# Norms, statistics and low parts in other places of the unit, one bias load a unit earlier, small modulation steps a unit later, in a fused attention and expert block

## The reference, cut to what matters

```python
h = _layernorm(x, axis=-1) * (1 + ca) + sa
q = (hs @ q_w.T + q_b).reshape(B, L, nh, d)        # k and v likewise
qn, kn = _l2norm(q / scale), _l2norm(k / scale)
gv = softplus(hs @ b_w.T + b_b)[..., None] * v
attn = einsum('bnhid,bnhjd->bnhij', qc, kc)        # chunks of 64 tokens
out = einsum('bnhij,bnhjd->bnhid', attn * mask, gvc)
x = x + ga * ((out * silu(hs @ og_w.T)) @ o_w.T + o_b)
h = _layernorm(x, axis=-1) * (1 + cb) + sb
x = x + gb * ffn(h)                                # 16 experts, top 6, and a shared one
```

## Time and profile before

| | |
|---|---|
| time of the kernel before, median of 3 runs | 2174.21 us (2173.03 to 2174.24) |
| the profiled execution's own time | 2172.59 us |
| its span, first to last instruction | 2170.9 us |
| PE busy | 2119.8 us (98%) |
| DVE, ACT, POOL busy | 1193.1 us (55%), 1030.9 us (47%), 525.2 us (24%) |
| mean granted clock of PE | 0.999 |
| the 128 attention units | from about 18 to 1317 us |

### The profile page before, as it was taken

One profiled execution on the slowest core, in us unless ns is written; L12 is line 12 of the kernel. 1 busy time (PEld: TensorE's weight loads), 2 busy tenths in 40 slices (PEclk: granted clock), 3 DMA queues, 4 the chain that ended last, 5 costly groups with the idle time before them and its releaser, 6 DMA issues.

```text
span 2170.9 us, 36048 instructions
## 1 busy us (share of the span) xinstructions
PE 2119.8 (98%) x12463; PEld 1751.7 (81%) x12463; DVE 1193.1 (55%) x2174; ACT 1030.9 (47%) x3301; POOL 525.2 (24%) x541
## 2 busy tenths in 40 slices
PE   7999999999999999999999999999999999999999
PEld 5877878887878887878888887888888888888887
DVE  5556556556556556556555454555555455545554
ACT  5655556566556556556555453333333232333322
POOL 2334344344343344344344441000000000000000
PEclk9999999999999999999999999999999999999999
DMA  7565333254355344445243130442334234223221
GB/s 258 173 225 205 115 120 130 79 161 141 81 142 157 92 164 106 114 139 161 93 142 114 54 127 31 142 168 103 127 110 150 101 112 163 103 90 119 93 97 63
DMA packets 191891, 274.79 MB, mean 127 GB/s; under 512 B 99184, under 2 KB 132960, under 8 KB 191712
## 3 DMA queue, kind: packets, MB, share of 16 engines
q1 hardware_dynamic: 191712, 272.49, 38.8%
HBM read 214.79 MB, written 57.67 MB: 126 GB/s over the span
## 4 chain that ended last, share of the span: by engine, by line
PE 88%; DVE 6%; issue 2%; ACT 2%; DMA 1%; POOL 0%; SPq 0%; DVEq 0%; ACTq 0%; POOLq 0%
PE proj_ps L664 47%; PE out_ps L664 14%; PE av_ps L891 4%; PE s_ps L879 3%; PE s_ps L939 3%; PE av_ps L939 3%; PE qt_ps L939 3%; PE kt_ps L939 3%; PE qt_ps L860 2%; PE kt_ps L865 2%; DVE gated_lo L1497 1%; DVE scores L1472 1%; DMA head_scr<-stage 1%; PE misc_ps L683 1%; DVE xn L1261 1%
## 5 line engine op out<-in xcount | busy, mean ns | idle before, releaser
L664 PE MATMUL proj_ps<-w_qkv,h_t 128*128 128x512 f32 x2304 | 617.6, 406 | 16.3 <-DVE q_sb L1464 5.7
L664 PEld LDWEIGHTS proj_ps<-w_qkv,h_t 128*128 128x128 f32 x2304 | 409.3, 189 | 107.9 <-issue 15.6
L664 PE MATMUL proj_ps<-h_t,w_qkv 128*128 128x512 f32 x1800 | 444.4, 391 | 0.1
L664 PEld LDWEIGHTS proj_ps<-h_t,w_qkv 128*128 128x128 f32 x1800 | 335.7, 188 | 69.2 <-issue 0.7
L621 POOL TENSOR_TENSOR inv_norm<-guarded,minus_half 128x8 f32<-128x8 f32 x128 | 209.9, 1639 | 730.3 <-DVE guarded L1481 730.3
L1182 ACT ACTIVATE w_gate<-v_sb 128x512 fp32r<-128x512 f32 x200 | 126.4, 632 | 314.5 <-DVE v_sb L1539 310.3
L1545 DVE TENSOR_TENSOR w_gate<-v_sb,w_gate 128x512 fp32r<-128x512 f32 x200 | 138.5, 693 | 139.4 <-ACT w_gate L1182 139.3
L1134 ACT ACTIVATE q_t<-qt_ps 128x512 f32<-128x512 f32 x128 | 76.1, 594 | 265.8 <-PE qt_ps L860 265.7
L1464 DVE TENSOR_TENSOR q_sb<-proj_ps,bias 128x512 f32<-128x512 f32 x128 | 88.4, 691 | 197.2 <-PE proj_ps L664 192.9
L664 PE MATMUL proj_ps<-h_t,w_gate 128*128 128x512 f32 x768 | 190.8, 399 | 3.8 <-ACT gate L1162 3.0
L1148 ACT ACTIVATE squares<-q_sb 128x128 f32<-128x128 f32 x512 | 151.4, 298 | 65.8 <-DVE q_sb L1464 60.7
(11 more groups left out here) (217 smaller groups left out, 3063.7 us busy)
## 6 DMA issues: line engine op xcount, KB each, us to landing
w_qkv<-tile_scr SPq DMA_DIRECT2D x100, 768.0 KB, 4.3
w_qkv<-head_scr SPq DMA_DIRECT2D x45, 1024.0 KB, 10.6
head_scr<-stage SPq DMA_DIRECT2D x30, 512.0 KB, 3.1
w_gate<-head_scr SPq DMA_DIRECT2D x15, 1024.0 KB, 5.0
w_out<-head_scr SPq DMA_DIRECT2D x15, 1024.0 KB, 4.9
tile_scr<-stage SPq DMA_DIRECT2D x25, 512.0 KB, 3.3
x_in<-_attn_hidden_states_dram SPq DMA_DIRECT2D x16, 512.0 KB, 6.3
h_scr<-stage SPq DMA_DIRECT2D x16, 512.0 KB, 3.4
```

What stands on the lines that cost most here:

```text
L664: mm = pe.matmul(out, w, y, start=(j == 0 and m == 0), stop=(3 * j + m == n - 1))
```

## The change

Five edits, with no arithmetic changed. (1) First norms of supertiles 2 to 7: the norm goes from `side[n+1, 0]` to `side[n+1, 1]`, its two transposes from (n+1, 1) and (n+2, 0) to (n+2, 0) and (n+2, 1), the split to (n+3, 0), beta to (n+3, 1), the next step to (n+4, 0); one chunk of later weights for each moves half a unit to a unit and a half earlier. (2) Routings of supertiles 0 to 5: the statistics go from (n+1, 1) to (n+2, 0) and the norm from (n+2, 0) to (n+2, 1). (3) On DVE a norm in `side[n, 1]` comes straight behind the guard, and at t = 1 both `lo_part` come behind it, instead of ahead of `side[n, 0]` and V's bias. (4) V's bias vector is loaded between the two halves of a group's last unit. (5) Only the copy of the second modulation stays in unit 1; its eleven small steps go to unit 2.

```diff
-            for (u, p), task in zip(((0, 0), (0, 1), (1, 0), (1, 1), (2, 0), (3, 0), (3, 1), (4, 0), (4, 1), (5, 0), (5, 1),
+            for (u, p), task in zip(((0, 0), (0, 1), (1, 0), (2, 0), (2, 1), (3, 0), (3, 1), (4, 0), (4, 1), (5, 0), (5, 1),
                                      (6, 0), (7, 0), (8, 0)), ROUTE):
...
-            first_norm(2 * (q + 1) + a, *((n + u, p) for u, p in ((0, 0), (1, 0), (1, 1), (2, 0), (2, 1), (3, 0), (3, 1),
+            first_norm(2 * (q + 1) + a, *((n + u, p) for u, p in ((0, 0), (1, 1), (2, 0), (2, 1), (3, 0), (3, 1), (4, 0),
                                                                   (4, 1), (5, 0), (5, 1), (6, 0), (6, 1))))
...
-                if r == 0 and gi:
-                    load_v_bias(gi)
...
                 for p in range(2):
+                    if p == 1 and r == 7 and gi + 1 < 4 * NG:
+                        load_v_bias(gi + 1)
                     for task in side[n, p]:
                         stores(task)
...
-            def late_modulation():
+            def copy_modulation():
                 dve.wait_ge(mod_turned, 2)
                 dve.tensor_copy(mod[:, 4:12, :], s_ps[:, 2 * P:4 * P].rearrange("p (r d b) -> p r d b", r=8, d=2)[:, :, 0, :])\
                    .then_inc(gained, 1)
+
+            def late_modulation():
...
-                if t == 1 and i:
-                    lo_part(n - 4)
-                    lo_part(n - 3)
                 for task in side[n, 0]:
                     do(task)
                 add_bias(n, V)
...
+                for task in side[n, 1]:
+                    if task[0] == "norm":
+                        do(task)
+                if t == 1 and i:
+                    lo_part(n - 4)
+                    lo_part(n - 3)
                 if n == 1:
                     for h in range(KC):
                         boot_part(O, h)
+                    copy_modulation()
+                if n == 2:
                     late_modulation()
                 for task in side[n, 1]:
-                    do(task)
+                    if task[0] != "norm":
+                        do(task)
```

## The result

The changed kernel takes 2141.70 us (median of 4 runs, 2140.01 to 2141.95), the kernel before 2174.22 (4 runs, 2173.03 to 2174.69) on the same chip: ratio 0.985, 95% interval 0.9833 to 0.9867, 32.5 us faster. The forecast was 2145. The profiled execution took 2141.68.

A forecast was written before the change was run, and what follows sets the result against it. PE, busy 98% of the 2170.9 us span, was taken as the bound, so only its waits count. Terms 7.0 + 1.9 + 4.4 + 1.3 + 3.9 + 6.4 = 24.9, plus 2.6 and 0.5, gave 28: 2145, range 2139 to 2150.

The forecast's parts named there:

- First norms, 7.0 and 1.9: Supertiles 2 to 7: PE's waits for xn fall from 10.4 to 3.4 us, 7.0 gained; gate matmuls behind them gain 1.9.
- The statistics, 4.4: Routings, six units and unit 9: PE's waits for Q's bias go except the one at the start, 4.4 us gained.
- the 0.17 each: Each PE wait that vanishes wholly gives 0.17 us beyond its bracket; some 15 waits, 2.6 us.
- V's bias earlier at t = 1, 1.3: At t = 1, five of six PE waits for V's bias vanish, 1.3 us gained.
- V's bias vector, 3.9: Units 24 and 8 to 10: earlier load removes 2.6 us of PE waiting and 1.3 of 1.7 at silu, 3.9 gained.
- Start, 6.4: Supertile 1's norm runs earlier: 5.4 us of PE waiting and 1.4 of slow clock go, 0.4 lost, 6.4 gained.
- The 0.4 us taken for a late Q bias: Unit 2: Q's bias comes at 35.0 to 35.7 us, PE wants V at 35.3, so 0.4 us is lost.
- Against: stores are issued by DVE's progress, so they move along.: Units 8 to 15: argument against DMAs giving back about 8 us when PE arrives some 7 us sooner; that case's chance 0.08.
- One of the prediction's own signs of being wrong: Units 8 to 15: the forecast is wrong if ACT waits longer for stage stores there; no size given.
- the rival on the DMAs: Units 8 to 15: store pace takes back the start's and unit 10's gain, about 8 us, giving 2153; chance 0.08.
- the end of the range with 1.2 us: Six norm units: if both low parts meet POOL's scaling of Q, they cost DVE 1.2 us in all.
- The slower case: Split and chunk ahead of V's bias at t = 3 make the next K wait, time about 2176; chance 0.02.

## Why the prediction was right

The size came out: 32.5 us faster where the text went from 2174 to 2145, and 30.9 by the spans where the sum was 28. The reading of most places was right, and it can be followed in the rows; but terms on both sides of the sum were off and partly met. By the blocks, statistics and V's bias at t = 1 gave 3.5 us more than their terms, the start, the vector's block and unit 10 together 2.0 more, and unit 14 took 2.3. That the time came out so near is in part luck: without the loss in unit 14 it would have stood near 2139.4, at the edge of the range.

- **First norms, 7.0 and 1.9.** Right to 0.5 us: five blocks gave 7.1 of 7.4. The waits left under `out_ps` are 3.1 in all against 3.4. But the 7.0 was put to the edits as a whole, and the runs show whose it is. With the table as before, the low parts' move gives 7.4 us at the six blocks and leaves waits for `xn` of 3.3; the table on top gives 2.0, the gates' 1.9 of the sum among them. So the projection that PE now does meanwhile, the prediction's reason, does not shorten the waits by itself. That the norm is no earlier in absolute terms holds for the pair only; with the low parts' move alone it is 1.3 us earlier.
- **The statistics, 4.4.** Under-sized: 6.9 at six places against 5.1 with the 0.17 each. The bracket of 0.77 stands for 1.02 from start to start, 0.25 more and not 0.17; and the gate blocks behind, which the term left out, fell by 0.07 to 0.10 at four units and by 0.36 and 0.40 at two.
- **V's bias earlier at t = 1, 1.3.** Mis-sized most: 4.4 us at twelve units against 2.7 with the small waits. I counted the waits that name V's bias. The lengthened gate blocks of units 38, 46, 70, 78, 102 and 110 belong to it as well (6.42 to 6.44 became 6.07 to 6.12 at four of them, 6.16 to 6.18 became 5.81 to 5.85 at two), as those waits go down under the silu. With the low parts undone the same blocks are at 6.43 to 6.45 and 6.17 to 6.18 again. In units 86 and 94 it is the counted wait (0.41 each, 0.35 and 0.33 gained). In units 54 and 62 (0.23 each) the view names no wait, but the next K started right behind V's bias before (574.70 and 574.65), and in the changed kernel V's bias is done 1.0 us ahead of it.
- **V's bias vector, 3.9.** Right: the load is issued at 259.37 and used at 268.80 without a wait. Undone it costs 2.9 by the medians: 4.6 at its places, of which 1.6 is the clock's, less 1.6 in unit 14.
- **Start, 6.4.** 7.1 came. The 0.4 us taken for a late Q bias did not arise, and the clock stayed up. The two edits there are each needed: undone, the one costs 4.9 at unit 2, the other 4.3, the fall of the clock behind the wait included (1.6 and 1.4). The prediction had that fall at 1.4 in the kernel before.
- **The wrong step: "Against: stores are issued by DVE's progress, so they move along."** Issuing moves along; landing does not. In unit 14 the store stood behind a 1 MB load that took 8.0 us instead of 5.0, and 2.3 us of lead went. One of the prediction's own signs of being wrong came with it: ACT's waits for stage stores in units 8 to 15 are 14.9 us, before 13.3. It is the rival on the DMAs, at a quarter of its price and in another unit than the one whose rows I had.
- **The low parts beside POOL.** At the first norms they take 1.29 for two, as before, so the end of the range with 1.2 us did not come into play. They do meet the scaling of Q, but the other way round: in unit 49 the second low part starts at 515.41 us and POOL's scaling at 515.50, and it is POOL's instruction that is longer, 1.50 where 1.04 stood. The price fell on an engine that had time.
- **The slower case** did not occur: no wait for K at t = 0 appears among PE's waits.

Left open: what made the 1 MB load of unit 13 take 8.0 us. The store behind it is held by it, and the load's move cures that, but the transfers ahead of the load were not varied, and the load's length differs (7.4 to 8.0 us) even among kernels that are alike up to there.

## What to carry to other kernels

When a releaser is named late, look at what stands ahead of it on its engine and whether that work is needed by then; here two low parts of 0.65 us each, wanted by nobody for several microseconds, stood ahead of a norm and a bias add that TensorE waited for, and that reordering alone gave 12.5 of 31 us. Where two edits shorten the same wait they don't add, as the low parts and the statistics here (0.30 and 1.14 us each alone, 1.14 together): price them together, and expect the second that is undone to look cheap. Before calling a shortfall an interaction, compare place by place: low parts and table added at each first norm, and it was another term that was mis-sized. An engine's work that comes sooner does not make its transfers land sooner: look for every large load issued just ahead of a store whose buffer is wanted soon.

## What the runs showed of the hardware

The norm's instruction on DVE (a tensor_scalar over 128x256 from one SBUF input) never took more than 417 ns before, and up to 1133 in the changed kernel. The tile's view, of before and of after (durations are minimum, median, maximum):

```profile
L1261 DVE TENSOR_SCALAR xn<-x_in,mean_var,rstd x64: 403/407/417, 8.1 to 1497.9; 128x256 f32<-128x256 f32 x64
```

```profile
L1261 DVE TENSOR_SCALAR xn<-x_in,mean_var,rstd x64: 400/407/1133, 8.2 to 1467.0; 128x256 f32<-128x256 f32 x64
```

Twelve of the 64 are long (1123 to 1133 ns). They are norms of routings, and start while POOL is already scaling Q (six) or V (six), which the guard just ahead of them started. Six more that had begun just before POOL's scaling of V kept 400 to 402 ns, and 28 beside POOL's inverse norm are at 401 to 412. DVE and POOL in unit 98 of the changed kernel:

```profile
1005.75 2.82 DVE L1261 TENSOR_SCALAR xn<-x_in,mean_var,rstd 128x256 f32<-128x256 f32 x4
...
1005.65 1.09 POOL L624 TENSOR_TENSOR q_sb<-q_sb,inv_norm 128x512 f32<-128x512 f32 x1
```

Four instructions that take 1.38 us elsewhere take 2.82. TensorE did not wait at this place, so it cost nothing here. The Trainium skill ("SBUF — State Buffer", Who interferes with whom) says that tensor_scalar can enter a mode in which it and GpSimd exclude each other for a whole instruction; the twelve agree, one scaling (1.04 to 1.09 us) waited out at a time. That the norm is in such a mode is not shown: at 407 ns it is no faster than a two-input subtraction of the same size (128x256, one input in PSUM, 411 ns). Who starts first matters in these rows: behind a low part that had begun up to 0.3 us earlier, POOL's scaling of Q takes 1.3 to 1.6 us, three times before and eleven times after; begun 0.5 us earlier, it leaves it at 1.1.

The granted clock fell behind idle stretches far shorter than the 5.4 us of the earlier trace rows, and the length of the wait alone does not say when. At the start it fell to 0.50 (40 to 42 us) behind 3.03 of idle time and stayed at 1.00 behind 3.02 in another kernel; in unit 24 it fell to 0.50 behind 2.67 and, in another, behind 1.78, and stayed at 1.00 behind 2.56 before; in unit 81 it fell to 0.61 (mean of 847 to 849 us) behind 2.04, and waits of 1.8 to 2.1 at four other first norms of that kernel left it at 1.00. At the start it was also 0.65 from 36 to 39 us behind 2.57. In the changed kernel the start shows no such fall. A fall cost about 1.0 to 1.6 us on top of the wait ahead of it. Each of these is one trace.
